# Queries split by sequence and ahead of the mask, score maxima in eleven rounds, transposes of exponentials spread between quarters

## The reference, cut to what matters

```python
x = x + L0_xattn(layernorm(x), ctx, ctx, mask)        # H = 16, D = 16
...
x = x + L1_xattn(layernorm(x), ctx, ctx, att_mask)    # one head, D = 256

def L0_xattn(q_vec, k_vec, v_vec, mask_input):
    q, k, v = heads(q_vec @ Wq.T + bq), heads(k_vec @ Wk.T + bk), heads(v_vec @ Wv.T + bv)
    energy = where(mask_input == 0, -1e9, q @ k.T / sqrt(16))
    return softmax(energy) @ v ... @ Wo.T + bo

def L1_xattn(q, k, v, att_mask):
    wq, wk, wv = q @ Wq.T + bq, k @ Wk.T + bk, v @ Wv.T + bv
    return softmax(wq @ wk.T / 16 + att_mask) @ wv
```

## Time and profile before

| | us |
|---|---|
| median of 3 runs | 1009.53 |
| lowest and highest | 1006.78, 1012.37 |
| profiled execution, its own time | 1008.83 |
| its span in the trace | 1007.0 |
| TensorE busy | 911.6 |
| VectorE busy | 604.2 |
| ScalarE busy | 479.5 |
| mean granted clock of TensorE | 0.961 of full |

### The profile page before, as it was taken

How to read it: one execution, slowest core, us unless ns; L and a number is a source line. 1 busy time by engine, 2 the same in 40 slices (tenths; PEclk the granted TensorE clock), 3 DMA queues, 4 the chain that set the end, 5 groups by cost and what they waited for, 6 DMA issues and landing times.

```text
span 1007.0 us, 15376 instructions
## 1 busy us (share of the span) xinstructions
PE 911.6 (91%) x6060; PEld 541.9 (54%) x6060; DVE 604.2 (60%) x1073; ACT 479.5 (48%) x951; POOL 105.7 (11%) x118
## 2 busy tenths in 40 slices
PE   6778899999999999999988899498999989988788
PEld 2344444444555555555444677354875854555656
DVE  5658587777875448888823686847414127188240
ACT  2322466777775557777787433223413110676111
POOL 3311011111000000000000100101000007155000
PEclk9989999999999999999999899678999989999889
DMA  9663843543422122223332500716508250000000
GB/s 358 167 203 126 251 117 101 152 138 115 131 64 75 32 54 64 74 64 113 121 121 96 213 1 1 251 42 217 222 26 321 93 167 1 1 1 2 0 1 21
DMA packets 66372, 108.68 MB, mean 108 GB/s; under 512 B 6902, under 2 KB 40438, under 8 KB 64374
## 3 DMA queue, kind: packets, MB, share of 16 engines
q1 hardware_dynamic: 64092, 100.35, 31.7%
q10 hardware_dynamic: 2208, 7.34, 1.8%
HBM read 93.77 MB, written 13.89 MB: 107 GB/s over the span
## 4 chain that ended last, share of the span: by engine, by line
PE 78%; DVE 8%; ACT 6%; issue 3%; DMA 3%; SPq 1%; POOL 0%; ACTq 0%; DVEq 0%
PE psum L1759 13%; PE psum L1741 10%; PE psum L1712 9%; PE psum L2116 6%; PE psum L2087 5%; PE psum L1876 5%; PE psum L1696 4%; PE psum L2179 4%; PE psum L1686 4%; PE psum L1889 3%; ACT arena L734 3%; DVE arena L1071 2%; DMA arena<-wvT 2%; PE psum L2227 2%; PE psum L2315 1%
## 5 line engine op out<-in xcount | busy, mean ns | idle before, releaser
L1071 DVE TENSOR_REDUCE arena<-psum 128x1 f32<-128x1024 f32 x256 | 300.6, 1219 | 111.3 <-PE psum L1712 111.2
L734 ACT ACTIVATE arena<-psum 128x512 f32<-128x512 f32 x512 | 264.5, 605 | 62.1 <-PE psum L1741 61.0
L1712 PE MATMUL psum<-arena 96*128 96x512 bf16 x512 | 151.5, 381 | 20.1 <-DVE arena L1071 11.3
L1741 PE MATMUL psum<-arena 99*128 99x256 bf16 x1024 | 160.2, 274 | 8.9 <-ACT arena L734 4.8
L1741 PEld LDWEIGHTS psum<-arena 99*128 99x128 bf16 x1024 | 79.5, 97 | 107.0 <-ACT arena L734 50.2
L1759 PE MATMUL psum<-arena 128*32 128x256 f32 x2048 | 136.8, 385 | 0.0
L1759 PEld LDWEIGHTS psum<-arena 128*32 128x32 f32 x2048 | 53.5, 109 | 75.4 <-ACT arena L734 36.9
L1686 PE MATMUL psum<-arena 128*128 128x512 f32 x128 | 65.0, 637 | 8.8 <-DMA arena<-ctxT 5.5
L1712 PEld LDWEIGHTS psum<-arena 96*128 96x128 bf16 x512 | 48.7, 98 | 38.9 <-DVE arena L1071 20.1
L627 POOL TENSOR_TENSOR arena<-arena 128x512 bf16<-128x512 f32 x34 | 41.6, 1223 | 206.7 <-DVE arena L1057 196.0
L1696 PE MATMUL psum<-arena 128*128 128x256 f32 x256 | 62.1, 387 | 0.0
(11 more groups left out here) (241 smaller groups left out, 972.9 us busy)
## 6 DMA issues: line engine op xcount, KB each, us to landing
arena<-kparts SPq DMA_DIRECT2D x192, 128.0 KB, 3.0
kparts<-arena SPq DMA_DIRECT2D x32, 384.0 KB, 3.3
arena<-ctxT SPq DMA_DIRECT2D x18, 512.0 KB, 5.4
arena<-ctx SPq DMA_DIRECT2D x2, 4096.0 KB, 15.3
arena<-mask SPq DMA_DIRECT2D x8, 1024.0 KB, 5.2
arena<-mask ACTq DMA_DIRECT2D x4, 1024.0 KB, 10.5
arena<-ctxT SPq DMA_DIRECT2D x1, 4096.0 KB, 14.1
arena<-ctxT SPq DMA_DIRECT2D x4, 1024.0 KB, 8.2
```

The source lines that it names most:

```text
L734: nc.scalar.activation(PR[step % 4][:, pair * CH:(pair + 1) * CH], ring_bank(slot), ACT.Exp)\
L1071: nc.vector.tensor_reduce(MX[g % 2][:, col:col + 1], unit_banks(n).rearrange("p b n -> p (b n)"), AX.X, ALU.max).then_inc(s_maxed, 1)
L1712: last = nc.tensor.matmul(out, q, KST[g % 2][0:ROWS, j, at], start=True, stop=not masked, skip_group_check=True)
L1741: last = nc.tensor.matmul(ring_heads(slot)[:, u, :], KST[gg % 2][0:KROWS, j, kc * P:(kc + 1) * P], QST[0:KROWS, G * g + j, b * S:(b + 1) * S],
```

## The change

- The queries are projected and split by sequence: `split_queries(b)` now takes both halves of the columns for one sequence b. Sequence 0 is piece 2, sequence 1 piece 5. A query piece is stored in three DMAs instead of one, and each sequence is loaded in six DMAs of 256 columns (512 B rows) instead of both in six of 512 columns. The loads for sequence 1 come in the step of chunk 4. `scores` waits for its own sequence's queries.
- VectorE splits the keys of chunks 0 to 2 and one piece of chunk 3 ahead of the flag, with the mask in two lots of four parts between them. `BRANCH` is 4. TensorE projects the first half chunk of values ahead of the branch.
- ScalarE's queue issues all four mask loads at the start. Context chunks 3 to 5 and the first row of ones are loaded from SyncE's queue, behind the weights. `cols` is loaded ahead of `x`. ScalarE copies the keys of chunk 0 ahead of the square root for the normalisation. `WQ` and `WV` have semaphores of their own.
- Units are spread over eleven rounds instead of twelve. Context chunk 6 is loaded one step earlier in SyncE's program.
- In the fourth layer `turn_exps(w, n)` and `copy_exps(w, n)` handle one group, `weigh_context(w, quarter)` one quarter, and each quarter raises `e_att`. Pairs of groups alternate with quarters on TensorE, and tile w + 1's first groups stand ahead of tile w's last quarter.

```diff
-BRANCH = 3
-EARLY = 2
-VALUES_AT = {3: 0, 4: 1, 5: 2, 6: 3, 8: 4, 9: 5, 10: 6, 11: 7}
-ROUNDS = 12
-UNITS_AT = {4: (2, 2), 5: (3, 3), 6: (3, 3), 7: (2, 2), 8: (2, 2), 10: (3, 3), 11: (2, 0)}
+BRANCH = 4
+VALUES_AT = {3: 0, 4: 1, 5: 2, 6: 3, 7: 4, 8: 5, 9: 6, 10: 7}
+ROUNDS = 11
+UNITS_AT = {4: (2, 2), 5: (3, 3), 6: (3, 3), 7: (3, 3), 8: (2, 2), 9: (3, 3)}
...
         def piece_number(b, c, f):
-            return 2 * NCH * b + 2 * c + f + (CT if b or c >= EARLY else 0)
+            return 2 * NCH * b + 2 * c + f + (2 if b else min(c, 2))
-        def query_piece(f):
-            return 2 * EARLY + f
+        def query_piece(b):
+            return 2 + 3 * b
...
+            for c in range(3, SLOTS):
+                sp.dma_start(CTX[c], ctx_chunk(0, c)).then_inc(ctx_loaded[c], 16)
+            sp.dma_start(arena[ROWS:KROWS, 0:8192], t["ones"]).then_inc(q_stacked, 16)
...
+            def store_queries(b):
+                r = query_piece(b)
+                sp.wait_ge(k_low, r + 1)
+                parts = KPT[place(r)].rearrange("p r (f n) -> p r f n", f=CT)
+                for part in range(3):
+                    sp.dma_start(qparts[part, :, b * S:(b + 1) * S].rearrange("(f p) n -> p f n", p=P), parts[:, part])\
+                      .then_inc(k_stored[place(r)], 16)
+            def load_queries(b):
+                r = query_piece(b)
+                stored(r)
+                for r in range(6):
+                    src = qparts[Q_PARTS[r], :, b * S:(b + 1) * S]
+                    sp.dma_start(QST[r:ROWS:6, :, b * S:(b + 1) * S], src.rearrange("(h d) n -> d h n", d=DH))\
+                      .then_inc(q_stacked, 16)
...
             for f in range(CT):
-                stored(query_piece(f))
-            for r in range(6):
-                sp.dma_start(QST[r:ROWS:6, :, :], qparts[Q_PARTS[r]].rearrange("(h d) n -> d h n", d=DH))\
-                  .then_inc(q_stacked, 16)
-            for c in range(EARLY, NCH):
+                store_k(0, 0, f)
+            store_queries(0)
+            for f in range(CT):
+                store_k(0, 1, f)
+            load_queries(0)
+            chunks_stored(0)
+            load_stack(0, 0)
+            store_queries(1)
+            for c in range(2, NCH):
...
+            copy_turned_x(0)
+            split_keys(0, 0, 0)
+            split_keys(0, 0, 1)
+            split_queries(0)
+            copy_turned_x(1)
+            split_keys(0, 1, 0)
+            split_keys(0, 1, 1)
+            for i in range(4):
                 mask_part(i)
-            split_queries(0)
-            dve.wait_ge(mask_counted, 1)
+            split_queries(1)
+            split_keys(0, 2, 0)
+            split_keys(0, 2, 1)
+            for i in range(4, 8):
+                mask_part(i)
+            split_keys(0, 3, 0)
+            dve.wait_ge(first_psum, 3)
...
-            def weigh_context(w, first=0, last_k=KC):
+            def weigh_context(w, quarter):
...
-                if last_k == KC:
-                    last.then_inc(on["e_att"], 1)
+                last.then_inc(on["e_att"], 1)
...
-            for w in range(2, 4):
-                turn_exps(w)
-                weigh_context(w)
+            for n in range(4):
+                turn_exps(2, n)
+            weigh_context(2, 0)
+            turn_exps(2, 4)
+            turn_exps(2, 5)
+            weigh_context(2, 1)
...
```

More of the change, by code:

```diff
@@ L429, in turn_at, with stores_by, stores_ahead @@
             return sum(place(n) == place(r) for n in range(r + 1))
+        def stores_by(r):
+            queries = sum(query_piece(b) <= r and place(query_piece(b)) == place(r) for b in range(B))
+            return 16 * (turn_at(r) + 2 * queries)
+        def stores_ahead(r):
+            return stores_by(max(n for n in range(r) if place(n) == place(r)))
         def load_number(b, c, again):
@@ L750, in _ @@
             act.wait_ge(cols_loaded, 16)
-            for c in range(ROUNDS):
+            copy_keys(0, 0, 0)
+            copy_keys(0, 0, 1)
+            act.wait_ge(ln_var, 1)
+            nc.scalar.activation(SD[:, 0:4], SD[:, 4:8], ACT.Sqrt).then_inc(ln_sd, 1)
+            for c in range(1, ROUNDS):
                 for i in range(2):
@@ L1158, in _ @@
             nc.vector.tensor_scalar(FLAG, FLAGF[0:1, 0:1], 0.0, None, ALU.is_lt).then_inc(mask_step, 1)
-            split_queries(1)
-            for c in range(EARLY, ROUNDS):
+            split_keys(0, 3, 1)
+            for c in range(BRANCH, ROUNDS):
                 for i in range(2):
@@ new lines, in project_queries_of @@
+            def project_queries_of(b):
+                pe.wait_ge(ht_ready, b + 1)
+                for f in range(CT):
+                    for c in range(CT):
+                        last = nc.tensor.matmul(psum[:, b, f * S:(f + 1) * S], WQ[:, c, f * P:(f + 1) * P],
+                                                HT[b][:, c * S:(c + 1) * S], start=(c == 0), stop=(c == CT - 1),
+                                                skip_group_check=True)
+                last.then_inc(first_psum, 1)
@@ L1833, in _ @@
+            project_keys(0, 3, 1)
             pe.wait_ge(built, 8)
@@ L2155, in _ @@
                     key_scores(w, n)
-            for w in range(2, 4):
-                turn_exps(w)
-                weigh_context(w)
+            for n in range(4):
+                turn_exps(2, n)
[3 more added lines that the diff above has]
+            weigh_context(2, 1)
+            turn_exps(2, 6)
+            turn_exps(2, 7)
+            weigh_context(2, 2)
+            turn_exps(3, 0)
+            turn_exps(3, 1)
+            weigh_context(2, 3)
+            turn_exps(3, 2)
+            turn_exps(3, 3)
+            weigh_context(3, 0)
+            turn_exps(3, 4)
+            turn_exps(3, 5)
+            weigh_context(3, 1)
+            turn_exps(3, 6)
+            turn_exps(3, 7)
+            weigh_context(3, 2)
+            weigh_context(3, 3)
             pe.wait_ge(on["e_masked"], 32)
```

256 lines of the change are left out of this document (134 added, 122 removed).

## The result

The changed kernel takes 1003.73 us (median of 20 runs, 999.96 to 1009.12) against 1010.27 for the kernel before (20 runs, 1006.40 to 1013.67): ratio 0.9952, with a 95% interval of 0.9936 to 0.9968. The medians lie 6.5 us apart, half of the forecast 12.9; the ratio stands for 4.8 us (3.2 to 6.5), a good third of it. The median lies 0.7 us outside the range of 989 to 1003.

The account below looks back on a forecast made before the run. TensorE is busy 91% of the span, so time can be had only where it waits. Gains of 6.2 (opening), 3.9 and 2.8 (query tiles) sum to 12.9 off 1008.8: 995.9, 996 for the median, range 989 to 1003.

Parts of the forecast that it names:

- wait for quarter 3: Opening, before unit 24: TensorE waits 3.9 us for the key stack's quarter 3, landing 12.5 us after the last keys.
- first unit at 45.0: Opening: the first unit of score maxima moves from 53.96 to 45.0, 9.0 us earlier.
- The normalised x is complete near 14.5: Opening, square root behind two key copies: normalised x ready near 14.5 instead of 12.5, two us late, hidden by key work.
- Rival 1: Opening: the loads hold the first unit back; with a start at 50 the gain falls to about 8, 1001; chance 0.15.
- The rounds: Opening, first unit to end of last keys: 37.3 us with eleven rounds, against 35.8 before.
- Clock behind that wait: Opening, after TensorE's idle before unit 24: half clock for some us, 1.5 us added.
- The shorter table of rounds gains nothing; it swaps values for a wait: Opening, last keys to turned scores: 28.05 us with eleven rounds against 28.2 before, so no gain.
- Tiles 2 and 3: Exponentials of query tiles 2 and 3: 38.44 us falls to 35.6, two hand-overs of 0.9 left; gain 2.8.
- Tiles 0 and 1: Query tiles 0 and 1: end moves from 745.05 to 741.3, with 1.75 charged for half clock; gain 3.9.
- The new wait: Query tiles 0 and 1: the copy of folded queries loses its cover, costing 0.45 us.
- Rival 4: Mixing stages, 550 to 750 us: the low clock level holds longer, 1016 at 40 us more of it; chance 0.03.

Follow-up runs that it names:

- x_first: The changed kernel with the load of `x` ahead of `cols` again, nothing else different; 998.73 us in a single execution.
- x_first_timed: The changed kernel with `x` loaded ahead of `cols`, run once more with 7 executions; 1005.04 us, ratio 0.9942 to the kernel before.
- x_even: The changed kernel with `x` loaded first, twelve rounds, and two units in each half of rounds 4 to 7; 994.02 us, ratio 0.9815 to the kernel before.
- x_even_copy: x_even with VectorE's copy of tile 0's second group of transposes ahead of `find_scale(2)`; 987.51 us, ratio 0.9778 to the kernel before.

## Why the forecast was wrong

The forecast gain was 12.9 us; the profiled span shows 6.0. The mechanisms of the fourth layer and of the wait for quarter 3 were right; the step that failed by most is the first unit at 45.0. By its own steps:

- **First unit at 45.0: failed, at "The normalised x is complete near 14.5".** I moved the square root behind two key copies and left the load of `x` where it was. The diff swaps the issues of `x` and `cols`, and I had priced that at nothing without saying so. The load landed 4.8 late. VectorE then had the normalised `x` at 17.3 instead of 14.5 and was idle 2.07 for the query product, where I had 0.6: 4.3 us together. Its own work was mis-sized as well: seven key splits took 11.5 us (10.3 forecast) and the eight mask parts 6.7 (5.85). With 0.4 more at the flag, the flag ended at 45.1 instead of 38.4. TensorE gave 2.0 back: the keys and values between flag and first unit ran at full speed, where I had charged that much for the clock. That leaves 49.86, 4.9 late.
- **With `x` first the 45.0 would have looked right, in part by luck.** In x_first the flag still ended at 40.8, 2.4 late by VectorE's longer work, and the unspent 2.0 of clock hid it: 45.54. The five other profiles with `x` first have 46.6 to 47.9. The loads held: the six loads of the queries were issued from 31.80 to 35.76 in the changed kernel, and nothing waited for them. Rival 1 had the right size (a start at 50) for the wrong reason.
- **The rounds: 37.3 us from first unit to the end of the last keys.** Measured 37.26.
- **The wait for quarter 3: right mechanism, mis-sized.** Landing at +14.6 instead of +12.5 (six issues 4.5 us instead of 3.0, landing 3.4 instead of 3.0): 2.1. The wait was 5.78 instead of 3.9. The +8.6 at which TensorE was to reach unit 24 was listed as two values halves and two waits for maxima; the timeline has three and one, and the sum came out near all the same (+8.8).
- **Clock behind that wait: 1.5 charged.** From unit 24 to the turned scores it took 18.30 where the forecast has 17.05 (28.05 - 12.5 + 1.5), so 1.25 more; and the half clock behind the turned scores was not in it at all: from there to the next keys it took 5.23 us (120.03 to 125.26) instead of 3.93, so 1.3 us.
- **"The shorter table of rounds gains nothing; it swaps values for a wait": wrong as a judgement, for it loses.** My own terms said so: with a warm first unit the old table needs 33.8 + 28.2 = 62.0 us to the turned scores, the new one 37.3 + 28.05 + 1.5 = 66.85. I had compared the part behind the keys alone. Those 4.85 us were in the sum, so they don't explain the miss; what the sum missed here is the 2.1 and 1.25 above. Measured: 62.95 with twelve rounds, 70.17 with eleven. In time it is 8 us (0.9871 against 0.9952), the largest loss in the kernel.
- **Tiles 2 and 3: 2.8 forecast, 2.7 measured.** The two hand-overs cost 0.34 and 0.23.
- **Tiles 0 and 1: 3.9 forecast, 2.7 measured.** The new wait is there (0.47 for 0.45). The fourth group took 0.88 to the first quarter's start, where I had 0.44, and the first quarter, mostly at half clock, 5.68 where one at full clock takes 3.62: 2.5 of clock charge together instead of 1.75, inside the bounds. Another 0.15 is a slip of mine, since 745.05 - 741.3 is 3.75 and not 3.9; the last 0.3 is in small waits. (The median had such a slip too: 995.9 and 0.7 make 996.6, not 996.)
- **Rival 4, the clock of the mixing stages, had 0.03 and deserved more as a spread.** In the profile of the changed kernel it worked the other way: 573.0 us from turned scores to first transposes against 575.5, with the clock at 1.00 in 550 to 560 and 0.83 before. Over the 20 executions of the changed kernel, a mean clock of 0.964 goes with a span of 998 to 1001 and 0.958 with 1006 to 1007, about 1 us for each 0.001, with a scatter of 3 us at one clock. Between kernels it can hide 4 us of a gain in the opening (x_first_timed, x_even). My range had no term for it.

The sum of the misses: opening 8.2 (4.9 + 2.1 + 1.25), tiles 0 and 1 1.2, tiles 2 and 3 0.1, the keys between them 0.1, less 2.5 from the stretch between opening and tile 0 and 0.2 at the end: 6.9, and 12.9 - 6.9 = 6.0, as measured. The 2.5 is luck as far as is known: over the 13 profiles this stretch takes 571.7 to 579.2 us, and TensorE's waits listed in it are not shorter than before (29.5 us against 28.3). Without it the span would show a gain of 3.5 us.

What stays open is why the clock comes back at different times in executions of one kernel, and what in the order ahead of the stretch makes one or the other more frequent. In x_first and x_first_timed TensorE's waits listed between turned scores and first transposes add up to 29.6 and 29.3 us, so their length does not explain it; no run here moved that stretch alone.

## What to carry to other kernels

When a table of rounds is shortened, compare the whole way from one fixed event to the next under both tables, at the same clock; a comparison that begins in the middle hides what the first half pays. Price every moved DMA issue, even by half a microsecond at the start of the program, where both queues' loads are in flight. And where the mean granted clock of single executions spreads by 0.005 or more, as here, take several executions and look at equal clocks too before a few microseconds are called gained or lost.

## What the runs showed of the hardware

- A 512 KB load issued at 1.72 us instead of 1.22 landed in 11.7 to 11.8 us (five profiles) instead of 7.3 to 8.0 (eight); a 45 KB load that took its place went from 7.8 to 8.5 down to 4.3 to 4.7. With two of four 1 MB mask loads issued only behind the first key copy it was still 11.8. The other queue's context loads landed 1 to 1.5 us sooner meanwhile (6.1 at the median, 7.6 in x_first). The Trainium skill, "DMA: Bandwidth & Descriptors", section "Queues, rings and completion order", says that a DMA engine takes packets in turn from the queues that have work. That the other queue's loads gain when `x` comes later fits it; the page gives no size. My estimate from the trace is 0.5 us for the later issue and 0.2 for 45 KB at the 256 GB/s of 2 to 4 us, 0.7 together; the trace shows 4.8, and no run here shows where the rest comes from.
- An issue of one DMA on SyncE's queue took 1.59 us once, where its neighbours take 0.56 to 0.60.
- Idle times of 2.75 to 5.8 us of TensorE were followed by 3.5 to 7 us at the lower clock level, 1.24 us mostly by none; in x_even a 1.24 and in x_even_copy a 1.25 was followed by half clock as well, so the idle time just ahead does not alone decide. The Trainium skill, "TensorE: Matmul & The Clock Gate", section "Part 1: The HAM clock gate", says that the level follows how busy the array has been. The windows agree as far as they show (0.50 behind 98 to 102, where the array was nearly unused); for the executions of one kernel that part behind equal waits they show no reason.
- The rows of 512 B of the query loads were no burden here: six loads were issued from 31.80 to 35.76, and the first unit, at 49.86 and in x_first at 45.54, waited for none of them. Their cost for each row was not measured.
